# A six-layer local-attention block on one core: exponential, norms and scaling moved half a step back, behind both squares

## The chip, the cores and the metric

The kernel runs on one core of a Trainium2 chip. TensorE (PE, with its weight loads as PEld), VectorE (DVE), ScalarE (ACT), GpSimd (POOL) and SyncE (SP, which starts the transfers) each work through a queue of their own, in the order in which it is written, and wait for each other by semaphores. The metric is the time of one execution on the device in microseconds (us). An execution of the kernel before took 3870.03 us (median of three runs).

## The reference, cut to what matters

Input is x of 8 batches, 512 tokens and 128 channels. It is normalised; from that, one causal attention (16 heads of 8) and a stack of six layers are computed, and the sum of both is added to x. A layer is a local attention and a gated MLP. The loop that the change touches is the local attention:

```python
q, k = l2norm(q) * qs, l2norm(k) * ksc          # 16 heads of 64, per token
q = q * cos * scale + rotate_half(q) * sin * scale
k = k * cos * inv + rotate_half(k) * sin * inv
sim = einsum('bhwie,bhwje->bhwij', bq, bk2) * 8  # 32 queries, 64 keys a window
sim = where(mask, -max, sim)
attn = softmax(sim, -1)
out = einsum('bhwij,bhwje->bhwie', attn, bv2)
return out.reshape(b, n, 1024) @ Wo
```

## The kernel before, in words

After the first normalisation and the causal part (to about 485 us of the span) a loop runs over six layers. In a layer the attention goes tile by tile: a tile is 128 tokens, 4 tiles a batch, 32 tiles in all. It is written as a software pipeline (`pipeline`, a function called once on each engine): 38 steps of a tile each, six written out, 24 in a loop over four at a time, eight written out. `behind(t, i, part, lag)` gives the tile that is `lag` steps behind the newest, or nothing where there is none. So in one step tile n is projected, tile n-1 turned, tile n-2 scored, tile n-3's softmax weights are turned and applied, and tiles n-4 to n-6 are projected out. 32 of the steps project, from the third on they score as well, and six at the end only drain.

A step has two halves, `wp` 0 and 1. A half works on two of the four blocks of 512 columns of a tile's q and k (c = 2wp and 2wp+1; blocks 0 and 1 are q, 2 and 3 are k), and on one of two groups of windows. The pieces of a half, with their lines:

- `project(c)` (PE, L401): three matmuls of 512 columns into one of two banks, `pj[c % 2]`.
- `square(c)` (ACT, L940): the squares of that bank; `rotate(c)` (DVE, L1257): its products with the rotary tables; `square_sums` (DVE, L1267): the sum of squares per head, over both blocks of the half.
- `norms` (ACT, L949, L952, L956): guard, logarithm and exponential of those sums, which gives the factors `rn`.
- `add(c)` and `scale(c)` (POOL, L1506 and L1520): the two rotary products added, then multiplied by `rn`.
- `turn_qk(c)` (PE, L614) transposes a block of the tile before into the bank `rbank`; `turned_qk(c)` (ACT, L790) copies it out, q blocks as two copies of 64 partitions, k blocks as one copy.
- `score(wp)` (PE, L401, 16 matmuls that the trace counts as 32, 128*64) adds the scores on top of a mask that lies in the bank `sbank`; `mask_ahead` (ACT, L790, the copy of `lmask` into a bank) puts it there; `shift(wp)` (DVE, L1277 and L1280) takes the maximum and subtracts it; `exp` (ACT, L983), `sums` (DVE, L1290, L1292) and `normalise` (POOL, L1529) make the weights.
- `turn_p` (PE, L645), `turned_p` (ACT, L790), `weigh` (PE, L401, 64*128), `weighed` (ACT, L790, 128x1024), `windows` (PE, L673, and an ACT copy) and `project_out` (PE, L401 with wvo) are the rest of the attention.

PE's order in a half is project(2wp), turn_qk(2wp), turn_p, project(2wp+1), score(wp), windows (half 0 only), weigh, turn_qk(2wp+1), project_out. Two of its waits matter: before score(wp)

```python
pe.wait_ge(S["masked"], g_of(bt) * 8 + 2 * tt + wp)
```

where S["masked"] counts the masks laid into the bank, one for each score; and, on ACT, before square(c)

```python
act.wait_ge(S["proj"], g + 1)
```

so a square waits for its own projection. On ACT the order of a half before the change is square(2wp), turned_qk(2wp), turned_p, square(2wp+1), windows and the heads of tokens (half 0), weighed, turned_qk(2wp+1), exp(wp), mask_ahead(wp), norms(wp).

Of the kernel before, what the change touches and what calls it, by code (L numbers as in the profile page):

```python
# [36 lines left out]
AREA = 25856  # L37
# [55 lines left out]
def build(nc, ins, out, layers=DEPTH):  # L93
    ctx = ExitStack()
    with ctx:
# [30 lines left out]
        rot = sb("rot", [TT, 2, 2, D])  # L126
# [23 lines left out]
        sqb, t12 = take(2, 512), take(2, 2, 512)  # L150
        qsum, qn = take(2, 512), take(4, 512)
# [4 lines left out]
        kT = take(HP, WIN + T)  # L156
        assert at[0] <= AREA

# [24 lines left out]
        assert at[0] <= AREA  # L183
# [115 lines left out]
        def _(sp):  # L299
# [6 lines left out]
            sp.dma_start(rot[:, :, :, :], ins["c_rot"]).then_inc(S["const"], 16)  # L306
# [56 lines left out]
            for l in range(layers + 1):  # L363
# [35 lines left out]
        def _(pe):  # L399
# [9 lines left out]
            pe.wait_ge(S["const"], 9 * 16)  # L409
# [143 lines left out]
            with pe.Fori(0, layers) as l:  # L553
# [14 lines left out]
                def step(t, i, part):  # L568
# [3 lines left out]
                    def join_weights():  # L572
# [6 lines left out]
                        pe.wait_ge(S["w_loaded"], (l + 1) * (5 * 16))  # L579
# [22 lines left out]
                    def turn_qk(c):  # L602
# [6 lines left out]
                        if c == 1:  # L609
# [3 lines left out]
                        for j in range(4):  # L613
                            m = nc.tensor.transpose(rbank[:, j * P:(j + 1) * P], qn[:, c, j * P:(j + 1) * P],  # L614
# [50 lines left out]
                    def windows():  # L665
# [5 lines left out]
                        pe.wait_ge(S["ev"], g * 4 + 1)  # L671
# [30 lines left out]
                    for wp in range(2):  # L702
# [5 lines left out]
                        if wp == 0:  # L708
                            windows()
# [78 lines left out]
        def _(act):  # L788
# [112 lines left out]
            def heads_of_weights(l):  # L901
                act.wait_ge(S["w_loaded"], (l + 1) * (5 * 16))
# [7 lines left out]
            with act.Fori(0, layers) as l:  # L910
# [11 lines left out]
                def step(t, i, part):  # L922
# [10 lines left out]
                    def square(c):  # L933
# [8 lines left out]
                    def norms(half):  # L942

                        if not (v := behind(t, i, part, 0)):
# [3 lines left out]
                        act.wait_ge(S["ssq_raw"], 2 * n + 3)  # L948
# [29 lines left out]
                    def exp(wp):  # L978
                        if not (v := behind(t, i, part, 2)):
# [5 lines left out]
                    def mask_ahead(wp):  # L985
                        if not (v := behind(t, i, part, 2)):
# [610 lines left out]
```

## Time and profile before

| what | value |
|---|---|
| median of three runs | 3870.03 us (3869.78 to 3876.5) |
| the profiled execution, its own time | 3872.81 us |
| its span, first to last instruction | 3871.0 us |
| PE busy | 92% |
| ACT, DVE, POOL busy | 78%, 76%, 64% |
| mean granted TensorE clock | 0.971 of full speed |

The span holds about 485 us ahead of the layers and six layers of some 563 us. Busy times are shares of the whole span; a line of the timeline gives the start of a group of instructions, its length, its engine and line, what it writes and reads, how many there are, and in brackets the idle time of the engine just before it with the engine that ended it. A line such as L790 or L401 is that of a helper which many pieces share, so the tiles and shapes tell them apart.

### The profile page before, as it was taken

What the parts mean: (1) busy time and instruction counts of PE and PEld (TensorE: products, weight loads), DVE (VectorE), ACT (ScalarE), POOL (GpSimd) and SP (SyncE); (2) the same over time, 40 slices, a digit from 0 to 9 for tenths busy, and PEclk for the clock granted to TensorE, in tenths of its full rate; (3) what the DMA queues carried; (4) which work ended last, traced back from release to release, by engine and by line L of the source; (5) the groups of instructions that cost most, each with busy time, mean ns of one, the idle gap of its engine ahead of it and who ended that gap; (6) DMA issues with size and microseconds to landing.
All of it is one profiled execution on the core that took longest, in us unless ns stands there. A gap on an engine that the chain in (4) does not pass through costs nothing.

```text
span 3871.0 us, 95171 instructions
## 1 busy us (share of the span) xinstructions
PE 3542.8 (92%) x30888; PEld 2679.4 (69%) x30894; DVE 2948.5 (76%) x4344; ACT 3021.4 (78%) x6096; POOL 2494.8 (64%) x2313
## 2 busy tenths in 40 slices
PE   5898679999889999889999899999799999799998
PEld 3444357777567777577777577776577777577776
DVE  4666378886788886788886788886788886788876
ACT  3556478887688887688887698886688886788885
POOL 3555377775377774577773577773677772677762
PEclk8999799999999999999999899999899999899999
DMA  4223200000100000000001000001000001000002
GB/s 134 86 91 94 55 2 1 0 0 1 30 2 0 0 0 22 9 2 0 0 0 30 2 2 0 0 0 30 2 1 0 0 1 29 2 1 0 0 1 72
DMA packets 59745, 67.76 MB, mean 18 GB/s; under 512 B 12006, under 2 KB 40164, under 8 KB 58468
## 3 DMA queue, kind: packets, MB, share of 16 engines
q1 hardware_dynamic: 59492, 64.64, 5.8%
q8 instruction: 128, 2.10, 0.2%
q14 instruction: 125, 1.02, 0.1%
HBM read 46.27 MB, written 18.35 MB: 17 GB/s over the span
## 4 chain that ended last, share of the span: by engine, by line
ACT 37%; issue 25%; PE 21%; DVE 12%; ACTq 2%; POOL 2%; DMA 1%; SPq 0%; DVEq 0%; POOLq 0%
PE bank L401 18%; ACT sb_area L790 18%; ACT bank L790 5%; DVE sb_area L1280 4%; ACT sb_area L940 4%; DVE sb_smax L1277 4%; ACT sb_lnb L952 3%; ACT sb_lnb L949 3%; ACT sb_area L983 2%; PE bank L673 1%; DVE sb_area L1155 1%; DVE sb_area L1257 1%; PE bank L614 1%; DVE sb_ssq L1267 1%; DMA sb_wqk_lo<-qk_rows 1%
## 5 line engine op out<-in xcount | busy, mean ns | idle before, releaser
L790 ACT ACTIVATE sb_area<-bank 128x512 f32<-128x512 f32 (+4 forms) x2149 | 1335.2, 648 | 209.4 <-PE bank L401 154.9
L1257 DVE TENSOR_TENSOR sb_area<-bank,sb_rots 128x1024 f32<-128x1024 f32 x768 | 939.1, 1225 | 393.7 <-ACT sb_area L940 392.9
L1520 POOL TENSOR_TENSOR sb_area<-sb_area,sb_rn 128x512 f32<-128x512 f32 x768 | 785.7, 1044 | 586.3 <-ACT sb_rn L956 586.3
L401 PE MATMUL bank<-sb_area 128*64 128x64 f32 (+6 forms) x17104 | 1062.2, 275 | 21.2 <-ACT bank L790 8.7
L1506 POOL TENSOR_TENSOR sb_area<-sb_area 128x512 f32<-128x512 f32 x768 | 969.4, 1280 | 86.6 <-DVE sb_area L1257 84.8
L401 PEld LDWEIGHTS bank<-sb_area 128*64 128x64 f32 (+4 forms) x17104 | 746.9, 145 | 283.1 <-issue 229.5
L401 PE MATMUL bank<-sb_wqk_hi,sb_xwin 128*128 128x512 f32 x1536 | 723.6, 473 | 55.7 <-DVE sb_xwin L1237 47.6
L401 PE MATMUL bank<-sb_area,sb_wvo 128*128 128x256 f32 x3072 | 728.3, 381 | 3.1 <-DVE sb_xT L1312 3.1
L401 PEld LDWEIGHTS bank<-sb_area,sb_wvo 128*128 128x128 f32 x3072 | 555.0, 190 | 78.4 <-issue 12.8
L614 PE MATMUL bank<-sb_ident,sb_area 128*128 128x128 f32 x3072 | 488.4, 282 | 39.9 <-ACT sb_area L790 31.2
L614 PEld LDWEIGHTS bank<-sb_ident,sb_area 128*128 128x128 f32 x3072 | 354.6, 143 | 235.6 <-issue 124.8
L940 ACT ACTIVATE sb_area<-bank 128x512 f32<-128x512 f32 x768 | 460.4, 600 | 29.6 <-PE bank L401 11.8
L1267 DVE TENSOR_REDUCE sb_ssq<-sb_area 128x16 f32<-128x1024 f32 x384 | 464.1, 1209 | 0.0
L1529 POOL TENSOR_TENSOR sb_area<-sb_area,sb_srec 128x512 f32<-128x512 f32 x384 | 400.9, 1044 | 85.5 <-DVE sb_srec L1292 85.5
L401 PE MATMUL bank<-sb_wqk_lo,sb_xwin 128*128 128x512 f32 (+4 forms) x1280 | 415.6, 406 | 28.4 <-POOL sb_xwin L1442 13.7
L401 PEld LDWEIGHTS bank<-sb_wqk_hi,sb_xwin 128*128 128x128 f32 x1536 | 300.9, 196 | 114.0 <-issue 52.6
L983 ACT ACTIVATE sb_area<-sb_area 128x512 f32<-128x512 f32 x384 | 243.3, 633 | 123.3 <-DVE sb_area L1280 116.6
L1290 DVE TENSOR_REDUCE sb_ssum<-sb_area 128x8 f32<-128x512 f32 x384 | 262.0, 682 | 45.6 <-ACT sb_area L983 40.3
L1280 DVE TENSOR_TENSOR sb_area<-bank,sb_smax 128x512 f32<-128x512 f32 x384 | 265.6, 692 | 13.3
L1277 DVE TENSOR_REDUCE sb_smax<-bank 128x8 f32<-128x512 f32 x384 | 261.7, 682 | 15.2 <-PE bank L401 15.2
L1155 DVE TENSOR_REDUCE sb_area<-bank 128x2 f32<-128x1024 f32 (+3 forms) x256 | 203.5, 823 | 83.5 <-PE bank L401 82.2
L401 PEld LDWEIGHTS bank<-sb_wqk_lo,sb_xwin 128*128 128x128 f32 (+1 forms) x1280 | 203.8, 197 | 77.1 <-issue 24.3
(115 smaller groups left out, 3979.4 us busy)
## 6 DMA issues: line engine op xcount, KB each, us to landing
qk_rows<-sb_p SPq DMA_DIRECT2D x52, 256.0 KB, 4.2
sb_wqk_hi<-qk_rows SPq DMA_DIRECT2D x32, 256.0 KB, 2.9
sb_wqk_lo<-qk_rows SPq DMA_DIRECT2D x32, 256.0 KB, 2.7
sb_area<-in_Wqkv SPq DMA_DIRECT2D x7, 1024.0 KB, 6.1
sb_area<-in_WvT SPq DMA_DIRECT2D x7, 512.0 KB, 7.4
sb_wo_bd<-in_Wo SPq DMA_DIRECT2D x14, 256.0 KB, 8.3
sb_area<-in_x SPq DMA_DIRECT2D x4, 512.0 KB, 6.1
sb_area<-in_x SPq DMA_DIRECT2D x8, 256.0 KB, 2.9
```

Of the source, the lines that this page charges most:

```text
L401: return nc.tensor.matmul(o, a, b, start=start, stop=stop, skip_group_check=True)
L614: m = nc.tensor.transpose(rbank[:, j * P:(j + 1) * P], qn[:, c, j * P:(j + 1) * P], ident[:, :])
L790: return nc.scalar.activation(o, i, ACT.Copy)
L940: nc.scalar.activation(sqb[:, c % 2, :], pj[c % 2][:, :], ACT.Square).then_inc(S["sq"], 1)
L983: nc.scalar.activation(dd[:, wp, :], dd[:, wp, :], ACT.Exp).then_inc(S["exp"], 1)
L1257: tt_(t12[:, c % 2, :, :].rearrange("p u (h d) -> p u h d", h=8), src, bc(rots[:, tt, s, :, :], [P, 2, 8, D], 2), ALU.mult).then_inc(S["ro ...
L1267: nc.vector.tensor_reduce(ssq[:, tt % 2, half, :], sqb.rearrange("p c (h d) -> p (c h) d", h=8), AX.X, ALU.add)\
L1277: nc.vector.tensor_reduce(smax[:, wp, :], s3, AX.X, ALU.max).then_inc(S["smax"], 1)
L1280: tt_(dd[:, wp, :].rearrange("p (h k) -> p h k", h=HP), s3, bc(smax[:, wp, :], [P, HP, 64], 2), ALU.subtract).then_inc(S["sub"], 1)
L1506: pt_(qsum[:, c % 2, :].rearrange("p (h e d) -> p h e d", h=8, e=2), t12[:, c % 2, 0, :].rearrange("p (h e d) -> p h e d", h=8, e=2), swap ...
L1520: pt_(qn[:, c, :].rearrange("p (h d) -> p h d", h=8), qsum[:, c % 2, :].rearrange("p (h d) -> p h d", h=8), r, ALU.mult).then_inc(S["qn"], 1)
L1529: pt_(dd[:, wp, :].rearrange("p (h k) -> p h k", h=HP), dd[:, wp, :].rearrange("p (h k) -> p h k", h=HP), srec[:, wp, :].unsqueeze(2).to_b ...
```

## The change

On ACT a half now runs square(2wp), square(2wp+1), then exp, norms of the half before, turned_qk(2wp), mask_ahead of the half before, turned_p, windows (now half 1) or the heads of tokens (half 0), weighed, turned_qk(2wp+1). On DVE `sums` goes behind both rotations. On POOL add(2wp) goes ahead of the two scales. On PE only `windows` moves, from half 0 to half 1. `sqb` has four places instead of two, so that a square needs not wait for the sums of the half before; the sums and the scaled values of q and k share one array `qn` of six places (`qk_place`), and `qsum` is gone. To make room, the rotary table `rot` is no longer kept but loaded again for every layer, in two transfers into the place of `kT` (two further increments of `w_loaded`).

```diff
-        sqb, t12 = take(2, 512), take(2, 2, 512)
-        qsum, qn = take(2, 512), take(4, 512)
+        sqb, t12 = take(4, 512), take(2, 2, 512)
+        qn = take(6, 512)
...
+        def qk_place(c, tt):
+            return c // 2 if c % 2 == 0 else 2 + c - 1 + tt % 2
...
+                for s in range(2):
+                    sp.dma_start(rot[s], ins["c_rot"][:, :, s, :, :]).then_inc(S["w_loaded"], 16)
...
-                        if c == 1:
+                        if c == 3:
                             pe.wait_ge(S["xwev"], g_of(bt) * 4 + tt + 1)
...
-                        if wp == 0:
+                        if wp == 1:
                             windows()
...
-                        act.wait_ge(S["ssq_raw"], g)
-                        nc.scalar.activation(sqb[:, c % 2, :], pj[c % 2][:, :], ACT.Square).then_inc(S["sq"], 1)
+                        act.wait_ge(S["ssq_raw"], g + 1 - c % 2)
+                        nc.scalar.activation(sqb[:, c, :], pj[c % 2][:, :], ACT.Square).then_inc(S["sq"], 1)
...
                     for wp in range(2):
                         square(2 * wp)
+                        square(2 * wp + 1)
+                        exp(3 - wp, 1 - wp)
+                        norms(1 - wp, 1 - wp)
                         turned_qk(2 * wp)
+                        mask_ahead(3 - wp, 1 - wp)
                         turned_p(wp)
-                        square(2 * wp + 1)
-                        if wp == 0:
+                        if wp == 1:
                             windows()
-                            if not (part == 0 and t == 0) and (v := behind(t, i, part, -1)):
-                                heads_of_tokens(*v)
+                        elif not (part == 0 and t == 0) and (v := behind(t, i, part, -1)):
+                            heads_of_tokens(*v)
                         weighed(4 - wp, 1 - wp)
                         turned_qk(2 * wp + 1)
-                        exp(wp)
-                        mask_ahead(wp)
-                        norms(wp)
...
-                        sums(3 - wp, 1 - wp)
                         rotate(2 * wp)
                         rotate(2 * wp + 1)
+                        sums(3 - wp, 1 - wp)
...
-                        pool.wait_ge(S["qn"], g + 5)
+                        if c % 2 == 0:
+                            pool.wait_ge(S["tr"], g)
...
+                        add(2 * wp)
                         scale(1 - wp, 2 - 2 * wp)
                         scale(1 - wp, 3 - 2 * wp)
                         normalise(3 - wp, 1 - wp)
-                        add(2 * wp)
                         add(2 * wp + 1)
```

ACT's queue in the last half that projects, before (from the copy of block 2 on; L940 is the square, L983 the exponential, the copy of sb_lmask the mask):

```order
L790 ACTIVATE sb_area<-bank 128x4x128 [waits s_tr]
L996 REGISTER_ALU
L997 REGISTER_ALU [waits s_pt]
L790 ACTIVATE sb_area<-bank 128x512 [waits s_yy]
L938 REGISTER_ALU
L940 ACTIVATE sb_area<-bank 128x512 [waits s_ssq_raw,s_proj]
L1005 REGISTER_ALU
L1006 REGISTER_ALU [waits s_yy]
L790 ACTIVATE sb_area<-bank 128x2x512 [waits s_oo]
L790 ACTIVATE sb_area<-bank 128x4x128 [waits s_tr]
L983 ACTIVATE sb_area<-sb_area 128x512 [waits s_sub]
L790 ACTIVATE bank<-sb_lmask 128x512
```

The same half with the change (L945 are the squares, L988 the exponential, L954, L957 and L961 the norms):

```order
L945 ACTIVATE sb_area<-bank 128x512 [waits s_ssq_raw,s_proj]
L943 REGISTER_ALU
L945 ACTIVATE sb_area<-bank 128x512 [waits s_ssq_raw,s_proj]
L988 ACTIVATE sb_area<-sb_area 128x512 [waits s_sub]
L953 ISA
L954 ACTIVATE sb_lnb<-sb_ssq,sb_guard 128x16 [waits s_ssq_raw]
L956 REGISTER_ALU
L957 ACTIVATE sb_lnb<-sb_lnb,sb_guard 128x16 [waits s_ssq]
L959 REGISTER_ALU
L961 ACTIVATE sb_rn<-sb_lnb 128x16 [waits s_qn,s_ln_part]
L795 ACTIVATE sb_area<-bank 128x4x128 [waits s_tr]
L795 ACTIVATE bank<-sb_lmask 128x512
```

The mask stood last but for the norms, at the end of the half ahead of the score that needs it; now it stands behind the second square, the exponential, the norms and a copy, in the score's own half.

PE's queue in the same half, from the second projection on, before (the matmuls of sb_area 64x64 are the scores):

```order
L401 MATMUL bank<-sb_wqk_hi,sb_xwin 128x512 [waits s_rotd,s_sq]
L401 MATMUL bank<-sb_wqk_lo,sb_xwin 128x512
L401 MATMUL bank<-sb_wqk_hi,sb_xwin 128x512
L401 MATMUL bank<-sb_area 64x64 [waits s_masked,s_ev]
L401 MATMUL bank<-sb_area 64x64 x15
L401 MATMUL bank<-sb_area 128x256 [waits s_yev,s_xwev,s_ptev]
L401 MATMUL bank<-sb_area 128x256 x3
```

and with the change:

```order
L406 MATMUL bank<-sb_wqk_hi,sb_xwin 128x512 [waits s_rotd,s_sq]
L406 MATMUL bank<-sb_wqk_lo,sb_xwin 128x512
L406 MATMUL bank<-sb_wqk_hi,sb_xwin 128x512
L406 MATMUL bank<-sb_area 64x64 [waits s_masked,s_ev]
L406 MATMUL bank<-sb_area 64x64 x15
L676 ISA
L678 MATMUL bank<-sb_ident,sb_xs 128x128 [waits s_ev]
L678 MATMUL bank<-sb_ident,sb_xs 128x128
L406 MATMUL bank<-sb_area 128x256 [waits s_yev,s_xwev,s_ptev]
L406 MATMUL bank<-sb_area 128x256 x3
```

The scores stand directly behind the second projection in both; only the two transposes of the windows came in behind them.

## Rows read from the trace of the kernel before

**Rows 1.** The page: busy times of the engines over the span.
```profile
PE 3542.8 (92%) x30888; PEld 2679.4 (69%) x30894; DVE 2948.5 (76%) x4344; ACT 3021.4 (78%) x6096; POOL 2494.8 (64%) x2313
```

**Rows 2.** By stretch: window, length, PE, PEld, DVE, ACT, POOL, PEclk, DMA, GB/s.
```profile
1632.92:1690.28 57.36, 45.21 (x459) 34.42 (x458) 47.42 (x67) 47.23 (x101) 44.07 (x40) 0.94 0.01 2
1690.28:2046.21 355.93, 348.20 (x3352) 279.46 (x3351) 303.46 (x438) 318.23 (x650) 276.65 (x252) 1.00 0.00 0
```

**Rows 3.** Timeline of PE: first projection of a layer's steps 7 and 32.
```profile
1690.22 0.58 PE L401 MATMUL bank<-sb_wqk_hi,sb_xwin 128*128 128x512 f32 x1
...
2046.21 0.58 PE L401 MATMUL bank<-sb_wqk_hi,sb_xwin 128*128 128x512 f32 x1
```

**Rows 4.** Timeline of PE, steady: projections, scores, windows, transposes.
```profile
2005.96 0.40 PE L401 MATMUL bank<-sb_wqk_hi,sb_xwin 128*128 128x512 f32 x1
2006.29 1.15 PE L401 MATMUL bank<-sb_area 128*64 128x64 f32 x32
2007.60 0.44 PE L673 MATMUL bank<-sb_ident,sb_xs 128*128 128x128 f32 x2 [0.15 <-ACT sb_area L790]
...
2011.08 0.58 PE L401 MATMUL bank<-sb_wqk_hi,sb_xwin 128*128 128x512 f32 x1
...
2011.97 0.60 PE L614 MATMUL bank<-sb_ident,sb_area 128*128 128x128 f32 x4
...
2013.63 2.22 PE L401 MATMUL bank<-sb_area 128*64 128x64 f32 x40
```

**Rows 5.** Timeline of ACT, steady: three copies, then exponential to next second square.
```profile
2006.36 1.80 ACT L790 ACTIVATE sb_area<-bank 64x512 f32<-64x512 f32 x3
...
2011.35 0.63 ACT L983 ACTIVATE sb_area<-sb_area 128x512 f32<-128x512 f32 x1
2011.89 0.58 ACT L790 ACTIVATE bank<-sb_lmask 128x512 f32<-128x512 bf16 x1
2012.48 0.31 ACT L949 ACTIVATE sb_lnb<-sb_ssq,sb_guard 128x16 f32<-128x16 f32 x1
2012.82 0.31 ACT L952 ACTIVATE sb_lnb<-sb_lnb,sb_guard 128x16 f32<-128x16 f32 x1
2013.16 0.22 ACT L956 ACTIVATE sb_rn<-sb_lnb 128x16 f32<-128x16 f32 x1
2013.40 0.60 ACT L940 ACTIVATE sb_area<-bank 128x512 f32<-128x512 f32 x1
2013.90 1.08 ACT L790 ACTIVATE sb_area<-bank 128x512 f32<-128x512 f32 x2
2014.85 0.62 ACT L940 ACTIVATE sb_area<-bank 128x512 f32<-128x512 f32 x1
```

**Rows 6.** Timeline of ACT and PE in the fill of the pipeline: scores that wait for their mask.
```profile
1647.80 0.58 ACT L790 ACTIVATE bank<-sb_lmask 128x512 f32<-128x512 bf16 x1
...
1648.53 1.15 PE L401 MATMUL bank<-sb_area 128*64 128x64 f32 x32 [0.60 <-ACT bank L790]
```

**Rows 7.** Busy time by stretch around two pauses of PE in the fill (columns as rows 2).
```profile
1648.50:1651.10 2.60, 1.15 (x32) 1.04 (x32) 2.00 (x5) 2.53 (x7) 1.74 (x2) 1.00 0.00 0
1651.20:1657.90 6.70, 5.63 (x19) 4.31 (x20) 5.05 (x9) 5.48 (x14) 4.40 (x5) 0.50 0.01 4
1622.80:1627.20 4.40, 0.85 (x4) 0.20 (x2) 2.86 (x5) 3.82 (x10) 3.71 (x4) 1.00 0.01 2
1627.30:1630.60 3.30, 3.20 (x12) 2.41 (x12) 2.38 (x3) 2.11 (x7) 1.81 (x3) 0.50 0.00 0
```

**Rows 8.** Timeline of PE at the lower clock: a first projection, transposes behind it.
```profile
1653.60 0.78 PE L401 MATMUL bank<-sb_wqk_hi,sb_xwin 128*128 128x512 f32 x1
...
1655.33 1.09 PE L614 MATMUL bank<-sb_ident,sb_area 128*128 128x128 f32 x4
```

**Rows 9.** DMA issues of the page: rotary table, per-layer scales, us to landing.
```profile
sb_qks<-in_qks SPq DMA_DIRECT2D x7, 128.0 KB, 8.1
...
sb_rot<-in_c_rot SPq DMA_DIRECT2D x1, 512.0 KB, 4.2
```

More of the change, by code:

```diff
@@ L36 @@
 MASKED = -1.0e30
-AREA = 25856
+AREA = 26880
 OUT_PARTS = (((6, 3), (5, 1)), ((5, 2), (4, 0)))
@@ L125, in build @@
         lng = sb("lng", [3])
-        rot = sb("rot", [TT, 2, 2, D])
         rots = sb("rots", [TT, 2, 2, D])
@@ L156, in build @@
         kT = take(HP, WIN + T)
+        rot = [kT[:, 4 + s, WIN:WIN + T].rearrange("p (t u d) -> p t u d", t=TT, u=2) for s in range(2)]
+        first_kept = at[0] - 4 * (WIN + T)
         assert at[0] <= AREA
@@ L182, in build @@
         xres = take(2, TT, C)
-        assert at[0] <= AREA
+        assert at[0] <= first_kept
         xb = ysum
@@ L407, in split3 @@
                 return mm(o, a_lo, b_hi, False, True)
-            pe.wait_ge(S["const"], 9 * 16)
+            pe.wait_ge(S["const"], 8 * 16)
             for b in range(B):
@@ L670, in windows @@
                         g = g_of(bt) * 4 + tt
-                        pe.wait_ge(S["ev"], g * 4 + 1)
+                        pe.wait_ge(S["ev"], g * 4 + 3)
                         for wp in range(2):
@@ L938, in square, with norms @@
                         act.wait_ge(S["proj"], g + 1)
-                        act.wait_ge(S["ssq_raw"], g)
-                        nc.scalar.activation(sqb[:, c % 2, :], pj[c % 2][:, :], ACT.Square).then_inc(S["sq"], 1)
-                    def norms(half):
-                        if not (v := behind(t, i, part, 0)):
+                        act.wait_ge(S["ssq_raw"], g + 1 - c % 2)
+                        nc.scalar.activation(sqb[:, c, :], pj[c % 2][:, :], ACT.Square).then_inc(S["sq"], 1)
+                    def norms(lag, half):
+                        if not (v := behind(t, i, part, lag)):
                             return
@@ L976, in turned_qk, with exp @@
                         m.then_inc(S["ev"], 1)
-                    def exp(wp):
-                        if not (v := behind(t, i, part, 2)):
+                    def exp(lag, wp):
+                        if not (v := behind(t, i, part, lag)):
                             return
@@ L983, in exp, with mask_ahead @@
                         nc.scalar.activation(dd[:, wp, :], dd[:, wp, :], ACT.Exp).then_inc(S["exp"], 1)
-                    def mask_ahead(wp):
-                        if not (v := behind(t, i, part, 2)):
+                    def mask_ahead(lag, wp):
+                        if not (v := behind(t, i, part, lag)):
                             return
@@ L1109, in _ @@
             column = iter(range(28))
-            for name, n in (("sq", 1), ("rotd", 1), ("ssq_raw", 1), ("add", 1), ("tr", 3), ("score", 2), ("yy", 2),
+            for name, n in (("sq", 1), ("rotd", 1), ("ssq_raw", 3), ("add", 1), ("tr", 3), ("score", 2), ("yy", 2),
                             ("pt", 2), ("qn", 6), ("ln_part", 3), ("pn", 1), ("oo", 1)):
@@ L1197, in prepare_weights @@
             def prepare_weights(l):
-                dve.wait_ge(S["w_loaded"], (l + 1) * (5 * 16))
+                dve.wait_ge(S["w_loaded"], (l + 1) * (7 * 16))
                 for c in range(4):
@@ L1205, in prepare_weights @@
                     for u in range(2):
-                        m = tt_(rots[:, :, s, u, :], rot[:, :, s, u, :], bc(qks[:, s, u, :], [P, TT, D], 1), ALU.mult)
+                        m = tt_(rots[:, :, s, u, :], rot[s][:, :, u, :], bc(qks[:, s, u, :], [P, TT, D], 1), ALU.mult)
                 m.then_inc(S["rots_ready"], 1)
@@ L1266, in square_sums @@
                         dve.wait_ge(S["ln_part"], g_of(bt) * 8 + 2 * tt + half)
-                        nc.vector.tensor_reduce(ssq[:, tt % 2, half, :], sqb.rearrange("p c (h d) -> p (c h) d", h=8), AX.X, ALU.add)\
+                        nc.vector.tensor_reduce(ssq[:, tt % 2, half, :], sqb[:, 2 * half:2 * half + 2, :].rearrange("p c (h d) -> p (c h) d", h=8), AX.X, ALU.add)\
                             .then_inc(S["ssq_raw"], 2)
```

20 lines of the change are left out of this document (9 added, 11 removed).

## The prediction

> **What bounds the kernel now.** The page comes first: PE is busy 92% of the span, the other engines 64 to 78% [rows 1]. By stretch, the six layers are alike, so one does for all. Its steps 7 to 32 are the steady part: 355.99 us for 25 steps, 14.24 us a step [rows 3]. Over the same stretch PE is busy 348.20 of 355.93 us [rows 2], which is 13.93 us a step: PE is all but full, and 0.31 us a step is all that a better order could give. The timeline of PE shows the same from near by: in a half the scores start at 2006.29, before the projection ahead of them has drained (2005.96 + 0.40 = 2006.36), and the one pause of the step is 0.15 us ahead of `windows` [rows 4]. ACT, with 318.23 of 355.93 us, has 1.5 us to spare in a step, DVE and POOL more [rows 2]. So what decides is whether PE ever has to wait, and for what.
>
> **The wait that the change makes.** The scores of a half need their mask in the bank. Before, ACT lays it at 2011.89 to 2012.47, and PE wants it at 2013.63 [rows 4, 5]: 1.16 us early, because it belongs to the half before. With the change the mask of a half stands on ACT behind that half's second square, and the count for which the scores wait is the same; so it is this very mask that they need. The second square waits for the second projection, and on PE the scores stand directly behind that projection. The queue therefore goes round once in every half: PE projects, ACT squares, exponentiates, takes the norms, copies a block, lays the mask, and only then may PE score. Behind the waiting scores on PE's queue stand windows, weigh, turn_qk, project_out and both projections of the next half; nothing overtakes them. Nothing else of PE's can fill the pause.
>
> Its length, from the starts of ACT's instructions one after the other [rows 5]:
> - projection ended to square begun: 0.05, an estimate; the two ends are 0 and the 0.15 of the last item here.
> - second square to the next instruction 0.50 (2013.40 to 2013.90); exponential 0.54 (2011.35 to 2011.89); norms 0.34, 0.34 and 0.24 (2012.48 to 2013.40).
> - the block's copy: one of 128x512 in half 1, 0.48 (two in the 0.95 from 2013.90 to 2014.85); two of 64 partitions in half 0, 1.20 (three in 1.80).
> - the mask itself 0.58, and 0.15 from its end to the first score, as where PE waited for a mask in the fill (1647.80 + 0.58 to 1648.53) [rows 6].
>
> That is 3.22 us in half 1 and 3.94 us in half 0. Before, the scores began 0.07 ahead of the projection's recorded end, so PE's sequence grows by 3.29 and 4.01, 7.30 us a step. A step is then 13.93 + 7.30 = 21.23 us, 6.99 more than 14.24.
>
> The Trainium skill, "ScalarE: Activation LUTs", section "Rules for kernel authors", budgets about 0.3 us for an ACTIVATE and 0.83 ns per element, 0.73 us where the rows show 0.48 to 0.60. By it the two pauses would be 1.65 us longer in sum, and the kernel would take about 6190 us. The rows are of these instructions themselves, so they decide.
>
> **The clock.** Twice in the fill of a layer PE pauses for some microseconds, and both times its clock is at the lower level of 1.2 GHz right behind: PE works 1.15 of 2.60 us and stands at 0.50 for the next 6.70 us; it works 0.85 of 4.40 us and stands at 0.50 for the next 3.30 us. In the steady part it stays at 1.00 [rows 2, 7]. At the lower level a first projection takes 1.73 us until the transposes behind it start (1653.60 to 1655.33) [rows 8], and 0.89 at the upper (2011.08 to 2011.97) [rows 4]: the work takes twice as long. The new pauses are 3.2 and 3.9 us, in each half, so I expect one fall in each half. It costs half of the working time that it covers: 1.7 us if 3.3 us of packed work are caught, 3.4 us if it is 6.7 us. The second stretch may begin within the pause, where it costs nothing; I take 2.3 us, the lower third, and keep both ends. A step is then 21.23 + 4.6 = 25.83 us, 11.59 more than now.
>
> The Trainium skill, "TensorE: Matmul & The Clock Gate", section "HAM oscillation — how this bites in real kernels", warns of just this: bursts of matmuls between waits that each start at half clock. It speaks against the change, and the two places of rows 7 agree with it; without it the sum would be that of the second rival.
>
> **The rest of the change.** Both squares together let `rotate` and the sums start earlier, norms and scales come half a step later; all of it lies beside PE's 21 us and more: POOL has 276.65 us of work in 25 steps, 11.1 a step, DVE 12.1 [rows 2], so a step of 25.8 covers them, and if PE did not wait they would still fit in 14.2. `windows` in half 1 waits for the copy that now stands ahead of the mask: no further wait. `weighed` and the odd copy come behind weigh while PE has project_out and a projection to do: covered as before. `rot` is loaded with the weights, while the MLP runs, and costs nothing in the six later loads; ahead of the first layer PE stands still for the last load (8.1 us to landing), and two transfers of 256 KB more (512 KB took 4.2) add 2 us, between 0 and 4 [rows 9].
>
> **The sum.** Of the 32 projecting steps 30 score. 26 of them are full: 6 x 26 x 11.59 = 1808 us. The four of the fill (steps 3 to 6) take 57.36 us now, of which PE works 45.21, some 3 us of that owed to the lower clock; 42 + 4 x (7.30 + 4.6) = 90, so 32 us more in each layer, 194 us. In the drain there is no projection, but norms and a copy now stand ahead of the mask for a half: 3 us a layer, between 0 and 5, 18 us. With the 2 us of the load: 2022 us. The profiled execution took 3872.8 us, so 5895; the median of the runs is 2.8 us lower: **5892 us**.
>
> **Rivals.**
> - **PE doesn't wait, and the change wins a little.** If the mask came in time, as it does now, the step would go down to what PE is busy, 13.93: 6 x 26 x 0.31 = 48 us less, and 3820 us where the fill gains a little too. It decides whether the mask is laid before PE ends the second projection. Against it stands the order of both queues; for it only that I misread which mask a count means. 2%; no change at all, 1%.
> - **The pauses don't bring the clock down.** 13.93 + 7.30: 6 x 26 x 6.99 = 1090, the fill 42 + 29.2 - 57.4 = 14 a layer (83), 20 for drain and load: 5065 us. For it: in the steady part PE's clock never fell [rows 2]. Against it: both places where a pause of some microseconds could be looked at [rows 7]. 7%.
> - **Only one of the two pauses brings it down**: a step of 23.53, 9.29 more: 1449 + 138 + 20, 5480 us. The shorter pause is in half 1. 15%.
> - **The lower clock lasts longer in each half**, 3.4 us lost: a step of 28.03: 2151 + 246 + 20, 6290 us. 7%.
> - **ACT's instructions don't overlap each other** behind a wait: at their recorded lengths (0.60, 0.63, 0.60 for square, exponential and copy) a half takes some 0.3 us more, 6 x 30 x 0.6 = 108: 6000 us. 8%. The Trainium skill's figures above would go the same way, and further.
>
> **How the numbers follow.** The forecast has 60%: 5892 us, and with a fall that costs 1.7 us in each half the same case ends at 5675. The range takes in that end, the case of one fall, ACT without overlap and most of the longer fall: 5450 to 6250 us; it leaves out the case without a fall and the faster one, and the top of the longest falls. A measurement of this kernel can tell some 0.2% from no change (8 us). Every case but the first rival is slower by far more: faster 2%, same 1%, slower 97%.
>
> **What would show it.** In the profile after: PE busy some 72% of the steady part (18.5 of 25.8 us) instead of 98%; a wait of PE for ACT's copy of the mask ahead of the scores in every half, 3.2 and 3.9 us long, some 360 of them, about 1300 us in all; that pair at the head of the list of waits and of the chain; the granted clock in the steady part near 0.8 instead of 1.00; ACT's second square waiting for PE; a steady step of 25.8 us. The pause alone shown, with the clock at 1.00, means the second rival. The prediction is wrong if the scores start right behind the second projection.

## The result and the profile after

The changed kernel takes **5439.62 us** (median of four runs, 5432.33 to 5446.67) against 3870.49 for the kernel before: 1.405 times as long, 95% interval 1.4025 to 1.4073. The forecast was 5892 us with a range of 5450 to 6250. The direction is right, the size is not: the measured time lies 452 us below the forecast and 10 us outside the range.

The page of the kernel after: its engines, and the group that waits most. These answer to [rows 1] (in the kernel after the line numbers behind the first functions are 5 or 6 higher, so L401 is now L406, the copies L795, the squares L945, the exponential L988):

```profile
PE 4008.2 (74%) x30894; PEld 3017.2 (55%) x30894; DVE 2990.0 (55%) x4346; ACT 3031.2 (56%) x6096; POOL 2495.4 (46%) x2313
...
L406 PE MATMUL bank<-sb_area 128*64 128x64 f32 (+6 forms) x17104 | 1332.9, 319 | 1205.3 <-ACT bank L795 1195.3
```

PE has hardly more to do than before (4008 us against 3543, and the difference is the lower clock), but 1205 us of idle time now stand ahead of the scores. The list of waits (us in all, times, longest):

```profile
POOL sb_area L1512 <- DVE sb_area L1262: 2071.4, 379, 16.1
PE bank L406 <- ACT bank L795: 1195.3, 366, 3.7
...
ACT sb_area L945 <- PE bank L406: 885.8, 727, 2.8
```

The second row is the one that matters: 366 waits for the mask, 3.7 us at most. The others follow from it: ACT's squares wait for PE, which waits for ACT's mask, and POOL's additions for DVE, which waits for those squares. POOL's 2071 us lead the list, where the forecast had the mask at its head; they are no cause, since the experiments below take the whole loss away with the order on POOL and DVE unchanged (e8).

By stretch, 40 halves of a layer's steady part (columns as in [rows 2]):

```profile
2342.58:2801.63 459.05, 325.34 (x2680) 257.27 (x2680) 245.39 (x351) 255.19 (x521) 221.37 (x200) 0.89 0.00 0
```

The stretch runs from one pair of POOL's scalings (L1526, one pair a half) to that 40 halves later, so 20 steps take 459.05 us: **22.95 us a step** where 25.83 was forecast. PE is busy 71% of it where it was 98%, and the mean granted clock is 0.89, not near 0.8. The steps are not alike, as the starts of three such pairs show, each two halves behind the last:

```profile
2652.92 2.04 POOL L1526 TENSOR_TENSOR sb_area<-sb_area,sb_rn 128x512 f32<-128x512 f32 x2 [0.35 <-ACT sb_rn L961]
...
2673.58 2.04 POOL L1526 TENSOR_TENSOR sb_area<-sb_area,sb_rn 128x512 f32<-128x512 f32 x2 [0.34 <-ACT sb_rn L961]
...
2697.43 2.04 POOL L1526 TENSOR_TENSOR sb_area<-sb_area,sb_rn 128x512 f32<-128x512 f32 x2 [0.35 <-ACT sb_rn L961]
```

A step of 20.66 us is followed by one of 23.85 us. Over the 20 steps the short ones come once in three or four. PE's timeline over two pauses:

```profile
2602.89 0.40 PE L406 MATMUL bank<-sb_wqk_hi,sb_xwin 128*128 128x512 f32 x1
2606.94 2.81 PE L406 MATMUL bank<-sb_area 128*64 128x64 f32 x40 [3.65 <-ACT bank L795]
...
2614.97 0.40 PE L406 MATMUL bank<-sb_wqk_hi,sb_xwin 128*128 128x512 f32 x1
2618.42 1.80 PE L406 MATMUL bank<-sb_area 128*64 128x64 f32 x32 [3.05 <-ACT bank L795]
```

They answer to 2005.96, 2006.29 and 2013.63 of [rows 4]: in the kernel before, the scores started ahead of the projection's end and now start 3.65 and 3.05 us behind it. What ACT does in the first pause, which answers to [rows 5]:

```profile
2603.33 0.60 ACT L945 ACTIVATE sb_area<-bank 128x512 f32<-128x512 f32 x1 [0.98 <-PE bank L406]
2603.82 0.62 ACT L988 ACTIVATE sb_area<-sb_area 128x512 f32<-128x512 f32 x1
2604.34 0.30 ACT L954 ACTIVATE sb_lnb<-sb_ssq,sb_guard 128x16 f32<-128x16 f32 x1
2604.67 0.31 ACT L957 ACTIVATE sb_lnb<-sb_lnb,sb_guard 128x16 f32<-128x16 f32 x1
2605.01 0.21 ACT L961 ACTIVATE sb_rn<-sb_lnb 128x16 f32<-128x16 f32 x1
2605.13 1.18 ACT L795 ACTIVATE sb_area<-bank 64x512 f32<-64x512 f32 x2
2606.21 0.58 ACT L795 ACTIVATE bank<-sb_lmask 128x512 f32<-128x512 bf16 x1
```

Second square, exponential, three norms, the block's two copies, mask, and 0.73 us after the mask's start the first score: the chain of the forecast, link by link.

The clock behind these two pauses, by stretch:

```profile
2603.40:2606.90 3.50, 0.00 (x0) 0.00 (x0) 2.23 (x4) 3.40 (x9) 2.87 (x3) 1.00 0.00 0
2606.90:2608.60 1.70, 1.66 (x36) 1.60 (x38) 0.47 (x1) 0.71 (x2) 1.70 (x3) 0.95 0.00 0
2608.70:2612.00 3.30, 3.30 (x14) 2.39 (x11) 1.94 (x3) 2.17 (x3) 0.87 (x1) 0.53 0.00 0
2612.10:2615.30 3.20, 3.20 (x19) 2.51 (x17) 1.47 (x3) 0.60 (x1) 0.00 (x0) 1.00 0.00 0
2618.50:2622.00 3.50, 3.50 (x40) 2.88 (x42) 1.71 (x3) 0.67 (x2) 3.14 (x3) 0.52 0.00 0
```

In the pause itself and in the 1.7 us of scores behind it the clock is still up (1.00, 0.95). Then it stands near 0.5, the lower level of 1.2 GHz, for 3.3 us, and is back for the next 3.2 us, before the next pause begins. Behind the second pause it falls almost at once when PE resumes (0.52 over 3.50 us). So a fall covers some 3.3 to 3.5 us of work and costs about half of that, 1.6 us: the long step has two, the short one none, and (23.85 - 20.66) / 2 = 1.6.

### The profile page after: what moved, and what is told of

The parts are those of the page before. It is cut to its first block, busy times and chain, and to the rows that moved or that the text cites. A ratio compares the mean times of both kernels' runs of the same rounds, so it can differ in the third digit from the quotient of the medians.

```text
span 5439.9 us, 94382 instructions
## 1 busy us (share of the span) xinstructions
PE 4008.2 (74%) x30894; PEld 3017.2 (55%) x30894; DVE 2990.0 (55%) x4346; ACT 3031.2 (56%) x6096; POOL 2495.4 (46%) x2313
## 4 chain that ended last, share of the span: by engine, by line
PE 60%; ACT 17%; issue 16%; POOL 3%; DVE 1%; ACTq 1%; DMA 1%; SPq 0%; POOLq 0%; DVEq 0%
PE bank L406 47%; PE bank L619 8%; ACT sb_area L795 5%; ACT sb_area L988 4%; ACT bank L795 3%; PE bank L650 3%; ACT sb_lnb L957 2%; PE bank L678 2%; ACT sb_lnb L954 1%; POOL sb_ptT L1552 1%; DVE sb_area L1160 1%; POOL sb_xwin L1552 0%; POOL sb_area L1512 0%; DMA sb_wqk_lo<-qk_rows 0%; ACT sb_area L945 0%
## 5 line engine op out<-in xcount | busy, mean ns | idle before, releaser
L406 PE MATMUL bank<-sb_area 128*64 128x64 f32 (+6 forms) x17104 | 1332.9, 319 | 1205.3 <-ACT bank L795 1195.3
L795 ACT ACTIVATE sb_area<-bank 128x512 f32<-128x512 f32 (+4 forms) x2149 | 1358.1, 645 | 1050.5 <-PE bank L406 638.4
L406 PEld LDWEIGHTS bank<-sb_area 128*64 128x64 f32 (+4 forms) x17104 | 941.8, 176 | 1530.9 <-ACT sb_area L795 1008.5
L945 ACT ACTIVATE sb_area<-bank 128x512 f32<-128x512 f32 x768 | 458.6, 597 | 888.2 <-PE bank L406 885.8
L1526 POOL TENSOR_TENSOR sb_area<-sb_area,sb_rn 128x512 f32<-128x512 f32 x768 | 784.5, 1042 | 149.7 <-ACT sb_rn L961 149.3
L406 PE MATMUL bank<-sb_area,sb_wvo 128*128 128x256 f32 x3072 | 799.1, 408 | 3.1 <-DVE sb_xT L1317 3.1
L406 PE MATMUL bank<-sb_wqk_hi,sb_xwin 128*128 128x512 f32 x1536 | 734.1, 479 | 54.6 <-DVE sb_xwin L1242 49.1
L406 PEld LDWEIGHTS bank<-sb_area,sb_wvo 128*128 128x128 f32 x3072 | 619.7, 213 | 96.8 <-issue 12.8
L619 PE MATMUL bank<-sb_ident,sb_area 128*128 128x128 f32 x3072 | 559.3, 312 | 51.1 <-ACT sb_area L795 40.4
L619 PEld LDWEIGHTS bank<-sb_ident,sb_area 128*128 128x128 f32 x3072 | 399.3, 157 | 295.4 <-issue 220.9
L406 PE MATMUL bank<-sb_wqk_lo,sb_xwin 128*128 128x512 f32 (+4 forms) x1280 | 422.8, 414 | 30.0 <-POOL sb_xwin L1447 13.8
L406 PEld LDWEIGHTS bank<-sb_wqk_hi,sb_xwin 128*128 128x128 f32 x1536 | 307.5, 200 | 110.3 <-issue 54.5
L406 PEld LDWEIGHTS bank<-sb_wqk_lo,sb_xwin 128*128 128x128 f32 (+1 forms) x1280 | 208.5, 202 | 80.2 <-issue 27.8
L988 ACT ACTIVATE sb_area<-sb_area 128x512 f32<-128x512 f32 x384 | 239.0, 622 | 0.1
```

Source lines behind the costliest of these rows:

```text
L406: return nc.tensor.matmul(o, a, b, start=start, stop=stop, skip_group_check=True)
L619: m = nc.tensor.transpose(rbank[:, j * P:(j + 1) * P], qn[:, qk_place(c, tt), j * P:(j + 1) * P], ident[:, :])
L795: return nc.scalar.activation(o, i, ACT.Copy)
L945: nc.scalar.activation(sqb[:, c, :], pj[c % 2][:, :], ACT.Square).then_inc(S["sq"], 1)
L988: nc.scalar.activation(dd[:, wp, :], dd[:, wp, :], ACT.Exp).then_inc(S["exp"], 1)
L1526: pt_(sums_of_heads, sums_of_heads, r, ALU.mult).then_inc(S["qn"], 1)
```

## The experiments

The table gives the times and the mean of a steady step of each kernel, worked out as above from POOL's scalings over 20 steps of one layer. The steady step is the sharper instrument, since it leaves the fill of the pipeline out. Where the clock falls now and then it differs a little from layer to layer (22.87 to 23.2 in the kernel after, 17.9 to 18.2 in e9).

| kernel | us, median | ratio to before, 95% interval | steady step, us |
|---|---|---|---|
| before | 3870 to 3873 | 1 | 14.23 |
| after | 5439.62 | 1.4025 to 1.4073 | 22.95 |
| e1_pause_filled | 5015.84 | 1.2935 to 1.2978 | 20.66 |
| e11_pause_half_filled | 5324.82 | 1.3721 to 1.3763 | 22.87 |
| e3_mask_behind_exp | 4571.14 | 1.1791 to 1.183 | 18.3 |
| e2_mask_first | 4060.41 | 1.0465 to 1.0506 | 15.33 |
| e4_mask_between | 4054.95 | 1.0452 to 1.0487 | 15.33 |
| e6_mask_on_dve | 4253.07 | 1.0958 to 1.1016 | 16.38 |
| e7_copies_between | 5581.42 | 1.4398 to 1.4458 | 23.90 |
| e9_before_mask_late | 4624.33 | 1.193 to 1.1978 | 18.1 |
| e8_mask_first_copies_between | 3826.94 | 0.9871 to 0.9916 | 14.02 |
| e10_before_windows_late | 3865.98 | 0.9971 to 0.9989 | 14.23 |
| e12_e8_windows_early | 3808.65 | 0.9826 to 0.9853 | 13.96 |

### What the lower clock costs

e1 puts work of no use into the pause: 20 transposes of the identity into a bank that the weighing overwrites anyway (the wait for that bank is left out of the lines below).

```diff
 project(2 * wp + 1)
...
+for j in range(20):
+    nc.tensor.transpose(ybank[j % 2][:, 0:P], ident[:, :], ident[:, :])
 score(wp)
```

> The changed kernel, with 20 transposes of the identity put on PE between a half's second projection and its scores, into the bank that weigh overwrites afterwards. Nothing else of the order changes. At the upper clock they take some 2.2 us (4 take 0.44), less than either pause (3.05 and 3.65 us in the profile after), so they lie inside it. Theory A, the pauses bring PE's clock down and that costs some 2.4 us a step on top of the pauses: the granted clock stays at 1.00 in the steady part, a step takes what a step without a fall takes, 20.7 us (10.44 + 10.22), and the time is 5440 - 6 x 26 x 2.4 less some 60 us of the fill, 5000 to 5080 us. Rival B, the clock is no cause and the longer halves are long for another reason: 5440 us as before, or more by what the transposes delay.

Measured: 5015.84 us, in the range of theory A and 424 us less than the changed kernel, with more work on PE. The timeline of PE in the two halves of a step, with the filler ahead of the first scores:

```profile
2607.90 2.35 PE L679 MATMUL bank<-sb_ident 128*128 128x128 f32 x20
2611.72 2.22 PE L406 MATMUL bank<-sb_area 128*64 128x64 f32 x40 [1.47 <-ACT bank L807]
...
2621.56 1.15 PE L406 MATMUL bank<-sb_area 128*64 128x64 f32 x32 [0.87 <-ACT bank L807]
```

and a steady stretch:

```profile
2170.00:2580.00 410.00, 363.78 (x3437) 312.03 (x3435) 243.76 (x348) 253.01 (x518) 219.23 (x198) 1.00 0.00 0
```

The scores still wait for the mask behind the filler (1.47 and 0.87 us), so the filler prolonged nothing; the granted clock is 1.00, and the step 20.66 us. This separates the two terms. The pauses alone make 20.66 - 13.93 = 6.73 us of a step. What is left up to 22.95 is the clock: **2.3 us a step**. The short step of the changed kernel, 20.66 us too, says the same.

e11 puts in 8 transposes instead of 20.

```diff
-for j in range(20):
+for j in range(8):
```

> The changed kernel with 8 idle transposes ahead of each scores instead of the 20 of e1_pause_filled: they take some 0.95 us of pauses of 3.65 and 3.05 us and leave 2.7 and 2.1 us idle; the wait for the mask is the same, so without any fall of the clock it gives 5016 us again. Theory A1 (what decides a fall is how long PE stands idle at one piece; at 1.7 us, in e3 and e9, a fall came about once in six halves, at 3.2 and 2.6, in e7, in every half): falls in part of the halves: 5100 to 5400 us. Rival A2 (any idle stretch over about 2 us has a fall): 5430 to 5600. Rival A3 (falls gone as soon as some work stands in the pause): 5010 to 5040.

Measured: 5324.82 us. The number is in the range of A1, but not for its reason. The scores' wait behind one filler of 1.03 us:

```profile
2347.82 1.78 PE L406 MATMUL bank<-sb_area 128*64 128x64 f32 x32 [2.18 <-ACT bank L807]
```

In the steady part 1.03 us of work in a pause changed next to nothing: 22.87 us a step, with the same pattern of long and short ones. Most of the 115 us were saved early in each layer: its 7th to 17th half take 113 us together, in the changed kernel 127 in three layers and 130 in the other three, some 95 us in all. So A1, by which shorter idle pieces bring fewer falls, is not borne out in the steady part.

### Where the mask stands

e3, e4 and e2 move the mask forward on ACT, e4 and e2 with the exponential ahead of it.

```diff
 square(2 * wp)
 square(2 * wp + 1)
 exp(3 - wp, 1 - wp)
+mask_ahead(3 - wp, 1 - wp)
 norms(1 - wp, 1 - wp)
 turned_qk(2 * wp)
-mask_ahead(3 - wp, 1 - wp)
```

That is e3, against the changed kernel. In e4 exponential and mask stand between the two squares, in e2 ahead of both.

> The changed kernel with the mask directly behind the exponential, ahead of norms and copy, still behind both squares. Theory A: the pause shrinks to 0.05 + 0.50 + 0.52 + 0.58 + 0.14 = 1.8 us in each half, a step to 13.93 + 3.7 = 17.7 us without a fall of the clock: 3873 + 6 x 26 x 3.4 = 4410 us. If the shorter pause brings the clock down as often as the longer ones, 2.4 us a step more: 4780 us. Rival C: hardly faster than 5440 us.

> The changed kernel with exponential and mask between the two squares of a half. Theory A: the mask is laid 0.50 + 0.54 + 0.58 = 1.6 us behind the first projection's end, which is when the second one ends (1.58 us later), so the scores wait some 0.2 us in a half: a step of 14.0 to 14.6 us, 3840 to 3940 us, no fall of the clock in the steady part. Rival C: above 4000 us.

> The changed kernel with ACT's exponential and mask put ahead of both squares of a half; norms, copies, squares, DVE, POOL and PE as changed. Theory A, all of the loss comes from the mask that stands behind the second square: the scores no longer wait, the clock stays up, the step falls to what PE is busy (13.93) or a little more, 3820 to 3890 us. Rival C, a good part of the loss is the half step by which exponential, norms, scales and sums come later (POOL waits 2071 us for DVE in the profile after): it stays above 4000 us.

Measured: e3 4571.14 us, between the 4410 of a kernel without falls and the 4780 of one with as many as before. Norms and copy no longer stand ahead of the mask, and the pauses are down to second square, exponential and mask:

```profile
2608.02 1.15 PE L406 MATMUL bank<-sb_area 128*64 128x64 f32 x32 [1.79 <-ACT bank L795]
...
2617.03 2.22 PE L406 MATMUL bank<-sb_area 128*64 128x64 f32 x40 [1.69 <-ACT bank L795]
```

The pauses are 1.79 and 1.69 us. Two halves without a fall take 17.65 us, and about one half in five (8 to 10 of 40 in a layer's steady part) is 1.6 us longer. The half ahead of the first of these rows is such a one; this is a stretch of it:

```profile
2600.00:2603.60 3.60, 3.60 (x24) 2.65 (x20) 2.78 (x5) 3.15 (x6) 3.60 (x4) 0.57 0.00 0
```

So pauses of 1.8 us bring a fall too (0.57 here), only more rarely.

e2 and e4 took 4060.41 and 4054.95 us. In e2 PE does not wait for the mask any more, in e4 for 0.2 us at most (246 times, 53.6 us in all), and the clock is at 0.97 in the mean, as before; but they are 188 and 182 us above the kernel before, where 3820 to 3890 and 3840 to 3940 were expected. The numbers are those of rival C, a loss by the half step that norms, scales and sums come later; e8 below shows that it is not that. The change costs something else that the pauses had covered. PE's list of waits in e2, and its timeline, show what:

```profile
PE bank L678 <- ACT sb_area L795: 169.3, 186, 2.0
PE bank L619 <- ACT sb_area L795: 149.9, 223, 2.6
```

```profile
2606.73 0.44 PE L678 MATMUL bank<-sb_ident,sb_xs 128*128 128x128 f32 x2 [0.87 <-ACT sb_area L795]
...
2615.48 0.63 PE L619 MATMUL bank<-sb_ident,sb_area 128*128 128x128 f32 x4 [0.50 <-ACT sb_area L795]
```

The windows of half 1 wait 0.87 us, and the odd transposes of half 0 wait 0.50, for the bank `rbank`. ACT copies its contents out behind the second square and the norms:

```profile
2604.81 0.60 ACT L945 ACTIVATE sb_area<-bank 128x512 f32<-128x512 f32 x1 [0.18 <-PE bank L406]
...
2606.10 1.06 ACT L795 ACTIVATE sb_area<-bank 128x512 f32<-128x512 f32 x2
```

Before, these copies stood between the two squares. The step is 15.33 us, 1.10 over 14.23, and 6 x 26 x 1.10 = 172 of the 188 us.

e6 takes the mask off ACT instead and lets DVE write it behind its subtraction.

```diff
 # ACT
 turned_qk(2 * wp)
-mask_ahead(3 - wp, 1 - wp)
 turned_p(wp)
...
 # DVE, in shift
+dve.wait_ge(S["sub"], m_ + 1)
...
+nc.vector.tensor_copy(sbank[:, :], lmask[:, 0 if first else 1, :]).then_inc(S["masked"], 1)
```

> The changed kernel with the mask written by DVE right behind its subtraction instead of by ACT; the order of all else stays. Theory A and D: scores no longer wait for the mask; the copies still stand behind the second square and the norms, so the step keeps 1.1 us of waits: 4030 to 4130 us. Rival H (DVE, 0.7 us busier in each half, becomes late with the rotations that the projections wait for): 4200 us or more.

Measured: 4253.07 us, in the range of rival H, but again not by its cause. DVE's rotations wait for ACT's squares (693 times, 427 us), and PE's list of waits has none for the rotations. PE's windows and odd transposes wait longer than in e2:

```profile
2650.24 0.44 PE L678 MATMUL bank<-sb_ident,sb_xs 128*128 128x128 f32 x2 [1.39 <-ACT sb_area L795]
...
2659.54 0.66 PE L619 MATMUL bank<-sb_ident,sb_area 128*128 128x128 f32 x4 [1.05 <-ACT sb_area L795]
```

They are 1.39 and 1.05 us instead of 0.87 and 0.50: 0.52 and 0.55 us more, and an exponential takes 0.52 to the next instruction. In e2 it stands ahead of the squares, in e6 between the second square and the copies. So the copies are late by just what stands ahead of them. The norms stand behind the exponential too, and POOL's scaling waits for them; most waits of the odd transposes are put down to that scaling:

```profile
PE bank L619 <- POOL sb_area L1528: 159.2, 144, 2.6
```

Copies and scaling are ready at nearly the same time there, 1.0 us late either way, and e6 does not tell which of them would suffice. The windows wait for the copies alone.

e9 is the test from the other side: the kernel before, with the mask alone moved behind the second square.

```diff
 square(2 * wp + 1)
+mask_ahead(3 - wp, 1 - wp)
...
 exp(wp)
-mask_ahead(wp)
 norms(wp)
```

> The kernel BEFORE with one line moved: the mask of a half is laid half a step later, behind the second square; all else as before. Theory A (the mask behind the squares makes PE wait at every scores): the second square ends about 0.7 to 2.3 us behind the second projection, the mask takes 0.58 us more, so pauses of 1.5 to 3.0 us in each half, 3 to 5.5 us per step of 14.24, and some falls of the clock: 4350 to 4900 us. Rival C (it takes the whole change, the mask alone is hidden): under 4000 us.

Measured: 4624.33 us, in the range of theory A. One moved instruction costs 20%. PE waits 1.88 and 1.75 us for it, and now and then the clock falls, in 5 to 8 of 40 halves; the third row is 300 us of a layer's steady part, with the granted clock at 0.97:

```profile
2647.52 1.59 PE L401 MATMUL bank<-sb_area 128*64 128x64 f32 x32 [1.88 <-ACT bank L790]
...
2657.99 2.22 PE L401 MATMUL bank<-sb_area 128*64 128x64 f32 x40 [1.75 <-ACT bank L790]
...
2700.00:3000.00 300.00, 241.32 (x2220) 192.56 (x2218) 205.05 (x290) 209.87 (x433) 182.45 (x166) 0.97 0.00 0
```

### Where the copies stand

e7 is the changed kernel with the copies back between the squares, the mask still last.

```diff
 square(2 * wp)
+turned_qk(2 * wp)
+turned_p(wp)
 square(2 * wp + 1)
 exp(3 - wp, 1 - wp)
 norms(1 - wp, 1 - wp)
-turned_qk(2 * wp)
 mask_ahead(3 - wp, 1 - wp)
-turned_p(wp)
```

> The changed kernel with only the copies (turned queries, keys, weights) back between the two squares: square, copies, square, exponential, norms, mask. Theory A (the path second square, exponential, norms, mask sets the pause, and what stands ahead of the second square lengthens it where it pushes this square back): the copies leave the stretch ahead of the mask (-1.1 us in half 0, -0.5 in half 1) but now push the second square back by up to 1.7 and 1.2 us; pauses of 2.5 to 4.2 us, 5100 to 5650 us. Rival G (where the copies stand is a cost of its own in the changed kernel too, 1.1 us a step): 5270 us or less with pauses unchanged at 3.65 and 3.05.

Measured: 5581.42 us, in the range of theory A. But the pauses are shorter than in the changed kernel, not longer:

```profile
2641.47 3.99 PE L406 MATMUL bank<-sb_area 128*64 128x64 f32 x40 [3.19 <-ACT bank L795]
...
2653.44 1.56 PE L406 MATMUL bank<-sb_area 128*64 128x64 f32 x32 [2.56 <-ACT bank L795]
```

They are 3.19 and 2.56 us, against 3.65 and 3.05. The copies did not push the second square back, as the expectation had it; with PE's pauses ACT has no backlog, and the square in half 1 begins 0.03 us behind the projection's end (2650.48 + 0.40):

```profile
2650.48 0.40 PE L406 MATMUL bank<-sb_wqk_hi,sb_xwin 128*128 128x512 f32 x1
```

```profile
2650.91 0.60 ACT L945 ACTIVATE sb_area<-bank 128x512 f32<-128x512 f32 x1
```

Without a fall a step would be 13.93 + 3.19 + 2.56 = 19.7 us (an estimate), and it is 23.90. Here every half has a fall, and that of half 0 begins inside the pause and lasts twice as long:

```profile
2638.30:2640.60 2.30, 0.00 (x0) 0.00 (x0) 1.33 (x2) 2.24 (x6) 1.27 (x1) 0.94 0.00 0
2640.70:2647.40 6.70, 5.93 (x48) 4.81 (x49) 3.40 (x6) 2.71 (x6) 4.28 (x4) 0.52 0.00 0
2653.50:2657.30 3.80, 3.80 (x42) 2.78 (x42) 2.33 (x4) 0.38 (x1) 3.66 (x4) 0.56 0.00 0
```

The clock costs 4.2 us a step, where it costs 2.3 in the changed kernel with its longer pauses.

e8 is e2 with the copies back between the squares: exponential, mask, square, copies, square, norms. The lines are against the changed kernel.

```diff
+exp(3 - wp, 1 - wp)
+mask_ahead(3 - wp, 1 - wp)
 square(2 * wp)
+turned_qk(2 * wp)
+turned_p(wp)
 square(2 * wp + 1)
-exp(3 - wp, 1 - wp)
 norms(1 - wp, 1 - wp)
-turned_qk(2 * wp)
-mask_ahead(3 - wp, 1 - wp)
-turned_p(wp)
```

> The changed kernel with the exponential and the mask at the head of each half (as in e2_mask_first) and, new, the copies of the turned queries and keys and of the turned weights back between the two squares; the norms stay behind the second square, half a step later than before, and the windows stay in half 1. Theory D: what e2 and e4 still lose against the kernel before (about 185 us, 1.1 us in each of 156 steps) is that these copies stand behind the second square and the norms, so that the bank they empty comes free late: PE then waits 0.87 us at the windows of half 1 and 0.50 us at the odd turn of half 0. If so, this kernel is back at the kernel before or slightly under it: 3820 to 3890 us. Rival E: the norms, half a step later, make POOL's scaling late, whatever the copies do: then 3980 us or more. Rival F: the sums of the weights behind the rotations on DVE: then also 3980 or more.

Measured: 3826.94 us, 1.1% **faster than the kernel before**. Theory D holds, E and F fall: norms and scaling half a step later, and the sums behind the rotations, stand in this kernel as in the changed one, and cost nothing that is not gained elsewhere. So of e2's 1.10 us a step the place of the copies is the cause.

### What makes e8 faster

Besides the order on ACT e8 still has the windows in half 1. e10 moves these alone in the kernel before; e12 moves them back in e8.

```diff
-if wp == 0:
+if wp == 1:
     windows()
```

That is e10, on PE and ACT, with the counts that go with it; e12 is the reverse, in e8.

> The kernel BEFORE with the turned windows moved from half 0 to half 1 on PE and ACT (with the counts they wait for), as the change has them; nothing else. Theory W: e8 is 1% faster than before because PE no longer waits for ACT's two copies of 64x512 ahead of the windows in half 0 (0.15 to 0.24 us in each step of before; in half 1 it is one copy of 128x512 that has to be done): 3825 to 3850 us. Rival X (that gain comes from the exponential, norms and scaling half a step later, which gives ACT and POOL slack): 3862 to 3880 us, no change. Rival Y (in half 1 ACT's second square is later, the windows wait longer there): 3890 or more.

> e8_mask_first_copies_between with the turned windows back in half 0, on PE and ACT, with the counts of the kernel before. e10 found 0.2% (some 7 us) for the windows alone, so most of e8's 1.1% should have another source. Theory X: it is the exponential and mask at the head of a half, and the norms and POOL's scaling half a step later, which no longer hold up ACT's squares: then 3830 to 3845 us, most of the gain stays. Rival W2 (the windows are worth more in e8 than alone, since there nothing else makes PE wait): 3855 to 3872 us, the gain goes.

Measured: e10 took 3865.98 us, in the range of X: 0.2% faster (0.9971 to 0.9989), with an unchanged steady step. e12 took **3808.65 us, 1.6% under the kernel before** and the fastest of all, below what either theory gave, since neither had the windows in half 1 down as a loss in e8. Its steady part and the rows that answer to [rows 4]:

```profile
1690.00:2046.00 356.00, 354.88 (x3442) 284.49 (x3439) 337.67 (x438) 315.32 (x654) 276.02 (x250) 1.00 0.00 0
```

```profile
2001.44 0.60 PE L619 MATMUL bank<-sb_ident,sb_area 128*128 128x128 f32 x4
...
2003.20 1.15 PE L406 MATMUL bank<-sb_area 128*64 128x64 f32 x32
```

```profile
2001.78 0.59 ACT L945 ACTIVATE sb_area<-bank 128x512 f32<-128x512 f32 x1
2002.26 1.80 ACT L795 ACTIVATE sb_area<-bank 64x512 f32<-64x512 f32 x3
```

PE is busy 354.88 of 356.00 us. The windows no longer wait, because ACT's copies begin 0.94 us ahead of the scores (2002.26 and 2003.20), where before they began 0.07 behind them (2006.36 and 2006.29 in [rows 4, 5]). In the kernel before, ACT had exponential, mask and three norms to do between two halves, and came to the first square late. The same half there, half 0, on PE and on ACT:

```profile
2004.62 0.60 PE L614 MATMUL bank<-sb_ident,sb_area 128*128 128x128 f32 x4
...
2005.87 0.60 ACT L940 ACTIVATE sb_area<-bank 128x512 f32<-128x512 f32 x1
...
2008.06 0.59 ACT L940 ACTIVATE sb_area<-bank 128x512 f32<-128x512 f32 x1
```

The first square begins 1.25 us after PE has gone on to the transposes behind that projection (2005.87 and 2004.62). In e12 the norms stand behind the second square, and the first square begins 0.34 us after those transposes (2001.78 and 2001.44). In the steady part that gives 6 x 26 x 0.27 = 42 of the 63 us. The rest, some 3.5 us a layer, lies mostly in fill and drain: by the same scalings a layer's first six halves are 1.0 to 1.7 us shorter, and the stretch from its 62nd half to the next layer 1.3 to 1.8. That the cause is the place of the norms is read from these rows; they were not moved alone in the kernel before, and the order of DVE's sums and POOL's additions differs as well.

## Why the prediction was wrong

- **"For this very mask they need", and the ring through ACT:** right. The wait stands ahead of 366 scores, in the place, the order and nearly the length that was forecast. That nothing overtakes the waiting scores is right too; e9 shows that the mask's place alone is enough.
- **The pauses:** 3.94 and 3.22 us forecast, 3.65 and 3.05 measured; 7.30 us a step with what the scores had been early, 6.73 by e1. Two links were a little shorter: the last norm hands on after 0.12 us instead of 0.24, and the two copies after 1.08 instead of 1.20. The 1.20 was two thirds of the recorded length of three copies and not, as the text says, from start to start: the next instruction begins 1.70 us behind the first copy (2006.36 and 2008.06 in the rows above), which gives 1.13. The 0.57 us a step that the pauses fell short are 89 us of the miss over 156 steady steps. The Trainium skill's budget for an ACTIVATE ("ScalarE: Activation LUTs", section "Rules for kernel authors"), 0.73 us by its figures for one whose bias is a pointer (an estimate), would have made the pauses still longer; here square and exponential handed on after 0.49 and 0.52.
- **"I take 2.3 us" for a fall, one in each half:** this is the step that failed, a term that was mis-sized. 4.6 us a step were forecast, 2.3 measured by e1 against the changed kernel; 6 x 26 x 2.3 = some 360 of the 452 us. Two things are in it. A fall costs 1.6 us, near the lower bound that the text had (1.7). And it does not come in each half: one step in three or four has none, so there are 2.3 / 1.6 = 1.4 falls a step where two were forecast. The forecast gave its two observed stretches of the fill as ends, took a value between, and held the frequency as certain. e7 shows that 4.2 us a step occurs as well, so the forecast value was not absurd; no row of the profile before shows which case holds. What the Trainium skill's "TensorE: Matmul & The Clock Gate" says in its section "HAM oscillation — how this bites in real kernels", bursts between waits that start at half clock, came true in part: the first burst behind the long pause ran 1.7 us at full clock.
- **"The pauses don't bring the clock down" (5065 us):** refuted as a cause, and confirmed as a sum: where the pauses are filled the kernel takes 5016.
- **"Only one of the two pauses brings it down" (5480 us):** near in time by luck and not in kind; falls come in both halves, in most of them, and each costs less.
- **"All of it lies beside PE's 21 us":** true of the changed kernel, and also the reason why a cost of 1.1 us a step stayed unseen. The text added that "if PE did not wait they would still fit in 14.2". That is wrong for the copies: with the mask in time the step is 15.33 (e2). With them back it is right (e8, e12).
- **Fill and drain:** 32 and 3 us a layer forecast. 5439.6 - 3870.5 - 156 x 8.72 = 209 us, 35 a layer: right as a sum. The forecast priced the falls of the fill at 2.3 us too, and its parts were not measured apart, so some luck may be in it.
- **The range:** its lower end was the case of one fall a step at 2.3 us. Cases of cheap falls in part of the halves, 1.7 each and not in all, were not among them; together with the slightly shorter pauses they lie near the measured time.

## What to carry to other kernels

When an engine writes something that another one needs at a fixed place of its queue, look at what stands between: here a 0.58 us copy, moved behind work that itself waits for the other engine, cost 20% alone, and in the changed kernel, with an exponential, three norms and a block's copy ahead of it too, 40%. Take such moves apart one by one: the same change held a gain of 1.1%, or 1.6% with the windows left in half 0 (most likely the norms half a step later, which were not moved alone), a loss of 1.1 us a step (copies out of a shared bank behind the norms) and the large loss that hid both. And price a fall of TensorE's clock by its frequency and its cost apart; here the clock cost between nothing (e1) and 4.2 us (e7) a step.

## What was not expected of the hardware

- A fall of the clock need not begin in the pause. In the changed kernel it began 1.7 us after PE had resumed (0.95 in 2606.90:2608.60, 0.53 in the next 3.3 us); in e7 it began in the pause and stayed for 6.7 us.
- Longer pauses are not dearer for the clock: pauses of 3.65 and 3.05 us lost 2.3 us of clock a step, those of 3.19 and 2.56 us lost 4.2. Pauses of 2.8 and 2.2 us with a burst of 1 us ahead of each (e11) lost the same as 3.65 and 3.05. Pauses of 1.7 to 1.9 us still brought falls, in about one half of five (e3) and one of six or seven (e9). What decides the beginning of a fall was not settled.
- Transposes of no use, 2.35 us of them in each pause, held the clock at 1.00 over 410 us of a layer's steady part and gave 424 us back, with 1.47 and 0.87 us of idle time still left behind them.
